# A Mamba block with a mixture of experts on one core: dt made by one Softplus activation in place of Abs, Relu, Exp, Ln and a GpSimd sum

## The reference

```python
xz = layernorm(x) @ W_in + b_in;  x_proj, z = split(xz)      # 256 and 256 channels
u = silu(x_proj)
B, C = split(u @ W_xproj + b_xproj)                          # 16 states each
dt = softplus(u @ W_dt + b_dt)                               # 256 channels
# for every channel d and state s, along the 512 steps:
h = h * exp(dt * A[d, s]) + (dt * u) * B[s]
y = sum_s h * C[s] + D * u
x = x + (y * silu(z)) @ W_out + b_out
# then softmax gates, top 2 of 8 experts and one shared expert, each
# silu(x @ w1.T) * (x @ w3.T) @ w2.T, scaled by its gate and summed; x = x + that
```

## Time and profile before

| | us |
|---|---|
| median of 3 runs | 1234.91 (1234.74 to 1237.38) |
| the profiled execution | 1235.3 |
| its span in the profile | 1233.3 |
| ACT busy | 1138.8 (92%) |
| PE busy | 1157.0 (94%) |
| DVE busy | 1130.1 (92%) |
| POOL busy | 1042.8 (85%) |

### The profile page before, as it was taken

The page is one execution under the profiler, slowest core; times in us unless marked ns, Lnnn a source line. Parts: engine busy times, 40 slices in busy tenths (PEclk is TensorE's granted clock), DMA queues, the critical chain, the costliest instruction groups (busy, mean ns, idle before and its releaser), DMA issues.

```text
span 1233.3 us, 21816 instructions
## 1 busy us (share of the span) xinstructions
PE 1157.0 (94%) x7200; PEld 946.7 (77%) x7200; DVE 1130.1 (92%) x1833; ACT 1138.8 (92%) x1982; POOL 1042.8 (85%) x534
## 2 busy tenths in 40 slices
PE   5466899999999999999999999999999999999998
PEld 3344576878888787878888787887878788888887
DVE  3788899999999999999999999999999999999754
ACT  6666999999999999999999999999999999989854
POOL 2999999999989999998999998999899899987300
PEclk8677999999999999999999999999999999999999
DMA  8333152506034160613325060433407043330000
GB/s 297 155 141 142 73 215 77 222 10 268 34 148 155 52 242 9 240 61 148 154 80 214 10 272 30 155 147 120 182 8 286 9 163 131 164 129 10 10 9 10
DMA packets 48016, 153.67 MB, mean 125 GB/s; under 512 B 4512, under 2 KB 29472, under 8 KB 31392
## 3 DMA queue, kind: packets, MB, share of 16 engines
q1 hardware_dynamic: 47904, 152.28, 31.9%
HBM read 147.03 MB, written 5.24 MB: 123 GB/s over the span
## 4 chain that ended last, share of the span: by engine, by line
ACT 50%; PE 26%; issue 10%; POOL 8%; DVE 4%; SPq 1%; DMA 1%; DVEq 0%; ACTq 0%; POOLq 0%
ACT da L661 13%; PE h L1021 13%; ACT L661 8%; ACT mixed L704 7%; ACT silu L697 6%; PE mixed L990 6%; PE y_acc L1003 5%; POOL dbu L754 4%; ACT L697 4%; DVE hc L856 3%; POOL hc L764 2%; ACT xn L677 1%; ACT xt L611 1%; ACT L642 1%; ACT lin L636 1%
## 5 line engine op out<-in xcount | busy, mean ns | idle before, releaser
L754 POOL TENSOR_TENSOR dbu<-w_s,b_all 128x1024 f32<-128x1024 f32 x256 | 604.3, 2383 | 2.1 <-DMA c_all<-bc_rows 2.1
L764 POOL TENSOR_TENSOR hc<-hc,c_all 128x1024 f32<-128x1024 f32 x128 | 304.6, 2380 | 92.0 <-DVE hc L856 91.6
L661 ACT ACTIVATE da<-dt_s,a_neg 128x512 f32<-128x512 f32 x512 | 342.1, 689 | 30.5 <-DVE hc L856 16.0
L1003 PE MATMUL y_acc<-ident,hc 128*128 128x128 f32 x2048 | 290.9, 279 | 35.8 <-POOL hc L764 25.0
L856 DVE TENSOR_TENSOR_SCAN hc<-da,dbu 128x512 f32<-128x512 f32 x256 | 302.2, 1211 | 18.6 <-ACT da L661 14.7
L856 DVE TENSOR_TENSOR_SCAN da<-da,dbu 128x512 f32<-128x512 f32 x256 | 308.1, 1216 | 10.4 <-POOL dbu L754 6.0
L1003 PEld LDWEIGHTS y_acc<-ident,hc 128*128 128x128 f32 x2048 | 246.5, 144 | 87.5 <-POOL hc L764 35.7
L990 PE MATMUL mixed<-w_s,g 128*128 128x128 f32 x2304 | 284.0, 276 | 4.6 <-DVE acc L906 1.8
L990 PEld LDWEIGHTS mixed<-w_s,g 128*128 128x128 f32 x2304 | 272.6, 192 | 20.0 <-DVE g L898 10.2
L1021 PE MATMUL h<-x_hi,w_hi 128*128 128x512 f32 x576 | 273.4, 475 | 9.6 <-ACT silu L697 6.2
L1021 PE MATMUL h<-x_hi,w_lo 128*128 128x512 f32 x576 | 228.2, 396 | 0.0
(11 more groups left out here) (79 smaller groups left out, 1039.3 us busy)
## 6 DMA issues: line engine op xcount, KB each, us to landing
b_all<-bc_rows SPq DMA_DIRECT2D x64, 1024.0 KB, 6.4
c_all<-bc_rows SPq DMA_DIRECT2D x64, 1024.0 KB, 8.8
xt<-in_x SPq DMA_DIRECT2D x16, 256.0 KB, 2.9
res<-in_x SPq DMA_DIRECT2D x16, 256.0 KB, 2.9
out<-acc SPq DMA_DIRECT2D x16, 256.0 KB, 4.3
silu<-in_w SPq DMA_DIRECT2D x6, 256.0 KB, 4.3
w_s<-in_w SPq DMA_DIRECT2D x1, 1152.0 KB, 7.3
bc_rows<-bc_rows_s SPq DMA_DIRECT2D x16, 64.0 KB, 1.6
```

Source lines behind the costliest of these rows:

```text
L661: act.activation(da[a % DA_SLOTS][:, :], dt_s[:, c, :], ACT.Exp, scale=a_neg[:, a:a + 1]).then_inc(decay_made, 1)
L754: pool.tensor_tensor(dbu[:, at:at + AT_ONCE, :], w_s[:, c, None, :].broadcast_to([P, AT_ONCE, T]), b_all[:, s:s + AT_ONCE, :], ALU.mult).t ...
L764: pool.tensor_tensor(pair, pair, c_all[:, s:s + 2, :], ALU.mult).then_inc(c_by_pool, 1)
L1003: last = pe.matmul(y_acc[:, b, :], hc[:, a % HC_SLOTS, b * P:(b + 1) * P], ident[:, :], is_transpose=True, start=False, stop=(a % NS == NS ...
```

## The change

Each half of dt is made by one Softplus activation out of the bank, straight into `dt_s`, which now has a slot for even and one for odd sequences. `softe`, `softl` and POOL's `dt` are taken out of all lists, the arrays `soft` and `lin` and three semaphores are gone, and nothing else is moved: `dlc.0` and `dlc.1` stand where they stood. Decays and w wait for the activation that frees the bank of `dl`. The activation waits (from sequence 2 on) until the sequence two before has made its decays and w of that half.

```diff
-        softe.0 decay.20-1 ycopy.0-1 decay.21-1 sc.5-3 softl.0 decay.22-1 decay.23-1 sc.6-3 bcc.0 decay.24-1
+        decay.20-1 ycopy.0-1 decay.21-1 sc.5-3 decay.22-1 decay.23-1 sc.6-3 bcc.0 decay.24-1
...
-        dbu.6+1 dbu.7+1 dt.1+1 w.1+1 rs2.0 hcp.10+1 dbu.8+1 dbu.9+1 hcp.14+1 dbu.10+1 hcp.18+1 dbu.11+1
-        dbu.12+1 dbu.13+1 dt.0+2 hcp.22+1 w.0+2 dbu.14+1
+        dbu.6+1 dbu.7+1 w.1+1 rs2.0 hcp.10+1 dbu.8+1 dbu.9+1 hcp.14+1 dbu.10+1 hcp.18+1 dbu.11+1
+        dbu.12+1 dbu.13+1 hcp.22+1 w.0+2 dbu.14+1
...
-        soft = sb("soft", [P, NC, T])
-        lin = sb("lin", [P, NC, T])
-        dt_s = sb("dt_s", [P, NC, T])
+        dt_s = sb("dt_s", [P, DT_SLOTS, NC, T])
...
                 elif what == "dlc":
-                    if not first:
-                        act.wait_ge(dt_made, NC * (m - 1) + a + 1)
-                    bias = bdt_s[:, a:a + 1]
-                    act.activation(soft[:, a, :], tile[:, :], ACT.Abs, bias=bias).then_inc(magnitudes, 1)
-                    act.activation(lin[:, a, :], tile[:, :], ACT.Relu, bias=bias).then_inc(freed, 1)
-                elif what == "softe":
-                    act.wait_ge(magnitudes, NC * (m + 1))
-                    act.activation(soft[:, :, :], soft[:, :, :], ACT.Exp, scale=-1.0).then_inc(soft_steps, 1)
-                elif what == "softl":
-                    act.wait_ge(soft_steps, 2 * m + 1)
-                    act.activation(soft[:, :, :], soft[:, :, :], ACT.Ln, bias=1.0).then_inc(soft_steps, 1)
+
+                    if m > 1:
+                        act.wait_ge(decay_made, STEPS * (m - 2) + NS * (a + 1))
+                        act.wait_ge(w_made, NC * (m - 2) + a + 1)
+                    act.activation(dt_s[:, m % DT_SLOTS, a, :], tile[:, :], ACT.Softplus,
+                                   bias=bdt_s[:, a:a + 1]).then_inc(freed, 1)
...
                 elif what == "decay":
-                        act.wait_ge(dt_made, NC * m + c + 1)
+                        act.wait_ge(*taken("dl", c, m))
...
-                elif what == "dt":
-                    pool.wait_ge(soft_steps, 2 * (m + 1))
-
-                    wait(pool, decay_made, STEPS * (m - 1) + NS * (a + 1))
-                    wait(pool, w_made, NC * (m - 1) + a + 1)
-                    pool.tensor_tensor(dt_s[:, a, :], soft[:, a, :], lin[:, a, :], ALU.add).then_inc(dt_made, 1)
                 elif what == "w":
-                    pool.wait_ge(dt_made, NC * m + a + 1)
+                    pool.wait_ge(*taken("dl", a, m))
```

More of the change, by code:

```diff
@@ L39 @@
 MIXED_BANKS, H_BANKS = 2, 3
+DT_SLOTS = 2
 SILU_SLOTS, G_SLOTS = 6, 3
@@ L120 @@
     "act": """
-        norm1.0 x_tc.0 u.0 u.1 whi.0 whi.1 whi.2 whi.3 bcc.0 whi.4 whi.5 dlc.0 dlc.1 softe.0 softl.0 whi.6
+        norm1.0 x_tc.0 u.0 u.1 whi.0 whi.1 whi.2 whi.3 bcc.0 whi.4 whi.5 dlc.0 dlc.1 whi.6
         whi.7 skip.0 whi.8 zs.0 decay.0 norm1.0+1 decay.1 decay.2 decay.3 decay.4 decay.5 decay.6 x_tc.0+1
         decay.7 decay.8 decay.9 zs.1 decay.10 decay.11 decay.12 decay.13 u.0+1 u.1+1 decay.14 decay.15
-        decay.16 dlc.0+1 decay.17 dlc.1+1 decay.18 ycopy.0 decay.19 softe.0+1 decay.20 softl.0+1 decay.21
+        decay.16 dlc.0+1 decay.17 dlc.1+1 decay.18 ycopy.0 decay.19 decay.20 decay.21
         decay.22 skip.0+1 bcc.0+1 decay.23 decay.24 decay.25 decay.26 decay.27 decay.28 decay.29 decay.30
@@ L128 @@
         decay.12+1 decay.13+1 silu.0 silu.1 u.0+2 u.1+2 silu.2 decay.14+1 decay.15+1 dlc.0+2 decay.16+1
-        dlc.1+2 decay.17+1 silu.3 decay.18+1 decay.19+1 ycopy.0+1 rexp.0 decay.20+1 softe.0+2 decay.21+1
-        softl.0+2 decay.22+1 decay.23+1 bcc.0+2 decay.24+1 decay.25+1 silu.4 silu.5 silu.6 silu.7 decay.26+1
+        dlc.1+2 decay.17+1 silu.3 decay.18+1 decay.19+1 ycopy.0+1 rexp.0 decay.20+1 decay.21+1
+        decay.22+1 decay.23+1 bcc.0+2 decay.24+1 decay.25+1 silu.4 silu.5 silu.6 silu.7 decay.26+1
         decay.27+1 skip.0+2 decay.28+1 decay.29+1 silu.8 decay.30+1 decay.31+1 sc.1 sc.2 decay.0+2 decay.1+2
@@ L134 @@
         sc.4 decay.12+2 decay.13+2 u.0+3 u.1+3 silu.15 silu.16 decay.14+2 decay.15+2 sc.5 decay.16+2 dlc.0+3
-        decay.17+2 silu.17 decay.18+2 bcc.0+3 decay.19+2 ycopy.0+2 decay.20+2 dlc.1+3 decay.21+2 softe.0+3
-        norm2.0+1 decay.22+2 decay.23+2 sc.6 decay.24+2 splitc.0+1 decay.25+2 xhi.0+1 softl.0+3 decay.26+2
+        decay.17+2 silu.17 decay.18+2 bcc.0+3 decay.19+2 ycopy.0+2 decay.20+2 dlc.1+3 decay.21+2
+        norm2.0+1 decay.22+2 decay.23+2 sc.6 decay.24+2 splitc.0+1 decay.25+2 xhi.0+1 decay.26+2
         sc.7 decay.27+2 decay.28+2 sc.8 decay.29+2 silu.0+1
@@ L167 @@
     "pool": """
-        rs1.0 resb.0 rs1.0+1 dt.0 dt.1 w.0 w.1 dbu.0 dbu.1 dbu.2 dbu.3 hcp.2 dbu.4 dbu.5 hcp.6 dbu.6 dbu.7
-        hcp.10 dbu.8 dbu.9 hcp.14 dbu.10 dbu.11 hcp.18 dbu.12 dbu.13 dbu.14 hcp.22 dbu.15 dt.0+1 hcp.26
+        rs1.0 resb.0 rs1.0+1 w.0 w.1 dbu.0 dbu.1 dbu.2 dbu.3 hcp.2 dbu.4 dbu.5 hcp.6 dbu.6 dbu.7
+        hcp.10 dbu.8 dbu.9 hcp.14 dbu.10 dbu.11 hcp.18 dbu.12 dbu.13 dbu.14 hcp.22 dbu.15 hcp.26
         w.0+1 rs1.0+2 dbu.0+1 hcp.30 dbu.1+1 dbu.2+1 dbu.3+1 hcp.2+1 dbu.4+1 rs2.0 dbu.5+1 hcp.6+1 dbu.6+1
[L171 to L175, removed]
+        w.1+1 hcp.10+1 dbu.7+1 dbu.8+1 dbu.9+1 hcp.14+1 dbu.10+1 rs1.0+3 hcp.18+1 dbu.11+1 dbu.12+1
+        dbu.13+1 hcp.22+1 dbu.14+1 w.0+2 hcp.26+1 dbu.15+1 dbu.0+2 hcp.30+1 dbu.1+2 dbu.2+2 dbu.3+2
+        hcp.2+2 resb.0+1 dbu.4+2 hcp.6+2 dbu.5+2 w.1+2 dbu.6+2 hcp.10+2 dbu.7+2 rs2.0+1 dbu.8+2
+        hcp.14+2 dbu.9+2 dbu.10+2 dbu.11+2 hcp.18+2 dbu.12+2 dbu.13+2 hcp.22+2 dbu.14+2 dbu.15+2
+        rs1.0+4 hcp.26+2 w.0+3 dbu.0+3 hcp.30+2 dbu.1+3 dbu.2+3 resb.0+2 hcp.2+3 dbu.3+3 dbu.4+3
         hcp.6+3 dbu.5+3 dbu.6+3 rs2.0+2 w.1+3 hcp.10+3 dbu.7+3 dbu.8+3 dbu.9+3 hcp.14+3 dbu.10+3 dbu.11+3
-        hcp.18+3 dbu.12+3 dt.0+4 w.0+4 dbu.13+3 hcp.22+3 dbu.14+3 dbu.15+3 rs1.0+5 hcp.26+3 dbu.0+4 dbu.1+4
-        hcp.30+3 dbu.2+4 dbu.3+4 dbu.4+4 resb.0+3 dt.1+4 hcp.2+4 dbu.5+4 hcp.6+4 w.1+4 dbu.6+4 dbu.7+4
-        rs2.0+3 hcp.10+4 dbu.8+4 dbu.9+4 dbu.10+4 hcp.14+4 dbu.11+4 hcp.18+4 dt.0+5 dbu.12+4 dbu.13+4
+        hcp.18+3 dbu.12+3 w.0+4 dbu.13+3 hcp.22+3 dbu.14+3 dbu.15+3 rs1.0+5 hcp.26+3 dbu.0+4 dbu.1+4
+        hcp.30+3 dbu.2+4 dbu.3+4 dbu.4+4 resb.0+3 hcp.2+4 dbu.5+4 hcp.6+4 w.1+4 dbu.6+4 dbu.7+4
+        rs2.0+3 hcp.10+4 dbu.8+4 dbu.9+4 dbu.10+4 hcp.14+4 dbu.11+4 hcp.18+4 dbu.12+4 dbu.13+4
         hcp.22+4 w.0+5 dbu.14+4
@@ L210 @@
         silu.14-4 silu.15-4 decay.14-2 decay.15-2 sc.4-4 decay.16-2 norm2.0-3 decay.17-2 dlc.0-1 decay.18-2
-        dlc.1-1 decay.19-2 ycopy.0-2 decay.20-2 softe.0-1 decay.21-2 sc.5-4 softl.0-1 decay.22-2 decay.23-2
+        dlc.1-1 decay.19-2 ycopy.0-2 decay.20-2 decay.21-2 sc.5-4 decay.22-2 decay.23-2
         sc.6-4 decay.24-2 bcc.0-1 decay.25-2 silu.16-4 sc.7-4 silu.17-4 decay.26-2 splitc.0-3 xhi.0-3
@@ L217 @@
         decay.13-1 u.0 silu.13-3 u.1 silu.14-3 silu.15-3 decay.14-1 decay.15-1 sc.4-3 decay.16-1 norm2.0-2
-        decay.17-1 dlc.0 decay.18-1 dlc.1 decay.19-1 ycopy.0-1 softe.0 decay.20-1 decay.21-1 sc.5-3 softl.0
+        decay.17-1 dlc.0 decay.18-1 dlc.1 decay.19-1 ycopy.0-1 decay.20-1 decay.21-1 sc.5-3
         decay.22-1 decay.23-1 sc.6-3 bcc.0 decay.24-1 decay.25-1 silu.16-3 sc.7-3 silu.17-3 decay.26-1
@@ L256 @@
     "pool": """
-        dbu.15-1 hcp.26-1 dbu.0 dbu.1 hcp.30-1 dbu.2 dbu.3 hcp.2 resb.0-1 dbu.4 dbu.5 hcp.6 dt.1 w.1 dbu.6
+        dbu.15-1 hcp.26-1 dbu.0 dbu.1 hcp.30-1 dbu.2 dbu.3 hcp.2 resb.0-1 dbu.4 dbu.5 hcp.6 w.1 dbu.6
         rs2.0-1 dbu.7 hcp.10 dbu.8 hcp.14 dbu.9 dbu.10 dbu.11 hcp.18 dbu.12 hcp.22 dbu.13 dbu.14 dbu.15
@@ L434, in build @@
         norm1_made = sem("norm1_made")
-        magnitudes = sem("magnitudes")
-        soft_steps = sem("soft_steps")
-        dt_made = sem("dt_made")
         w_made = sem("w_made")
@@ L660, in task @@
                             act.wait_ge(scanned, STEPS * (m - back) + user + 1)
-                    act.activation(da[a % DA_SLOTS][:, :], dt_s[:, c, :], ACT.Exp,
+                    act.activation(da[a % DA_SLOTS][:, :], dt_s[:, m % DT_SLOTS, c, :], ACT.Exp,
                                    scale=a_neg[:, a:a + 1]).then_inc(decay_made, 1)
@@ L731, in task @@
                                        ALU.add).then_inc(res_biased, 1)
-                elif what == "dt":
-                    pool.wait_ge(soft_steps, 2 * (m + 1))
-                    wait(pool, decay_made, STEPS * (m - 1) + NS * (a + 1))
-                    wait(pool, w_made, NC * (m - 1) + a + 1)
-                    pool.tensor_tensor(dt_s[:, a, :], soft[:, a, :], lin[:, a, :], ALU.add).then_inc(dt_made, 1)
                 elif what == "w":
-                    pool.wait_ge(dt_made, NC * m + a + 1)
+                    pool.wait_ge(*taken("dl", a, m))
                     pool.wait_ge(*taken("xp", a, m))
-                    pool.tensor_tensor(w_s[:, a, :], dt_s[:, a, :], u[:, a, :], ALU.mult).then_inc(w_made, 1)
```

(1 more changed line is left out.)

## The result

The change made the kernel slower: 1318.38 us median (1316.73 to 1318.58) against 1235.06, a ratio of 1.067 with a 95% interval of 1.066 to 1.068. Forecast were 1284.4 and a range of 1260 to 1302. The direction was right and so was the mechanism of the scans; the loss is 83 us where I had worked out 49.5.

A forecast was written before the change was run, and what follows sets the result against it. ACT's own work was taken to set the 70.97 us period. Window 41, sequence 15 3.5, sequences 1 to 4 10 and start -5 gave 49.5 on 1235.3: 1284.8, or 1284.4 beside the median; range 1260 to 1302.

The forecast's parts named there:

- the mechanism of the scans: Window: scans 18 and 19 wait 1.3 and 2.9 us for ACT's decays, leaving DVE 4.25 us late.
- (a): Window, sequences 5 to 14: each period grows by 4.1 us, 41 us in all.
- (b): Sequence 15: same lag of the scans, less DVE work between, estimated at 3.5 us.
- (c): Sequences 1 to 4: POOL's two saved sums pay for most of a lag; 0.4, 4, 3.3 and 2.6, 10 us.
- (d): Start, sequence 0: POOL's first w can start 5.7 us earlier; a gain of 5 us taken.
- Loads and Softplus: ACT, one dt: Softplus 0.68 us, two round trips with four loads; 6.7 to 6.8 us against 6.90 before.
- The lag: Window: scan 19 makes DVE 4.25 us late, then ACT idles 4.1 at decay.22 and decay.23; period 75.1 us.
- PE follows: Window: PE is late inside the same lag, as bc.0 needs the bank comb.5 leaves; no added cost.
- ACT's own work sets the period: Kernel before, window: ACT is never held up while DVE sometimes is, so ACT's work makes the 70.97 us.
- the ring: Window: ACT's decay.22 and decay.23 wait for DVE's mul.20 and mul.21, then ACT works 57.2 us without a wait.
- R1: Rival: DVE's lag is caught up and time follows ACT's sum of work, faster, 1228; chance 0.08.

The follow-up runs named there:

- e1: Changed kernel plus seven zero-weight multiplies on PE inside h3.14 in every sequence, filling PE's idle time: 1304.71 us, ratio 1.056.
- a1: Changed kernel with dlc.1 moved directly behind dlc.0 in all sequences but 3, one table round trip for two: 1265.44 us, ratio 1.024.
- b1: Changed kernel with DVE's g.12 moved ahead of scan.19, in the window's list alone: 1302.79 us, ratio 1.054.
- a2: Changed kernel with Abs in place of Softplus, so no table loads before it: 1233.04 us, ratio 0.998.
- e2: The a2 kernel with one of the three products of every expert unit left out on PE: 1219.39 us, ratio 0.988.
- b3: The b2 kernel with ACT's ycopy.0 moved ahead of dlc.1 in the window's list: 1301.97 us, ratio 1.054.
- b2: Changed kernel with DVE's g.12, g.13 and g.14 moved ahead of scan.19, in the window's list alone: 1300.89 us, ratio 1.053.

## Why the prediction was wrong in size

The growth of each interval from one `dlc.0` to the next, by step of the prediction:

| step | forecast us | measured us |
|---|---|---|
| (a) window, sequences 5 to 14 | 10 x 4.1 = 41 | 58.9 |
| (b) sequence 15 and what follows | 3.5 | 5.5 |
| (c) sequences 1 to 4 | 0.4 + 4 + 3.3 + 2.6 = 10 | 4.9 + 4.8 + 4.7 + 6.7 = 21.1 |
| (d) start | -5 | -2.3 |
| spans, 1316.5 - 1233.3 | 49.5 | 83.2 |

- **Loads and Softplus: right.** 0.687 us for a Softplus (0.68 taken), a load ahead of it and one at the decay behind, 1.30 and 2.0 us as steps, 29 loads more. The drain of about 1380 ns that the Trainium skill (ScalarE: Activation LUTs, What ACT_TABLE_LOAD costs) adds to each load is not seen here either: 1.29 us from the start of the load at 665.39 to the Softplus at 666.68.
- **The lag: right to a tenth.** Waits of 1.30 and 2.78 us at the scans, then ACT's at `decay.22` and `decay.23`. With PE's clock kept up (e1) the period is 75.12 for the 75.1 worked out, and with one round trip (a1) it is 72.86 for a lag of 1.87.
- **"PE follows": the step that failed.** I had PE late inside the same lag and gave it no price. It stops for 4.03 us at `h3.15`, whose bank `g.12` of DVE has to leave, comes back at half clock, is late with `eo.6`, and makes `g.15` wait, which stands ahead of `mul.21` in DVE's list and so on the very ring that sets the period. That is the term missing from (a): 1.8 us a sequence, shown by e1 and by the two periods of the changed kernel. Some two thirds of it pass through `g.15` (0.53 and 1.45 us of wait in turn). The other 0.5 us come after `decay.23`, most of it at `sc.7` of ACT, which waits 0.3 us for PE's product and waits for nothing in e1. The Trainium skill (TensorE: Matmul & The Clock Gate, Why this matters for your kernels) warns of idle gaps between bursts of multiplies, and the trace agrees: 0.50 behind 4.03 us.
- **(c), sequences 1 to 4: mis-sized.** I let POOL's saved sums pay for the lag at the start since POOL set the pace there. They did not: POOL itself now waits 3.09 us for scan 19 of sequence 0 (its `hcp.18` starts at 72.58 us), and is busy 35.41 of the 40 us from 40 to 80. In e1 these four intervals grow by 4.3, 3.1, 4.5 and 4.1 us, 5 less than here. Only sequence 4 (4.1 for 6.7) is the clock, which was at half here from 289 to 296 us and is not in e1. The other 2.4 e1 has lost ahead of them: both kernels reach the `dlc.0` of sequence 3 at 205 us. So of the 11 us missing 2.6 are the clock, and some 8.5, which e1 has too, are lag that I had discounted. The sizes in the first intervals are good to 3 us only: b1, whose edit lies in the window alone, reaches that `dlc.0` at 201.8.
- **(d), the start: mis-sized.** POOL's first dbu came 5.3 us earlier, but DVE's last weight subtractions took 2.06 us each beside POOL, where they had taken 0.64, and held the first scan (29.49 to 35.66). The price I allowed for was POOL's w being slow, not DVE. (b), the end, took 5.5 us for 3.5; that was not followed up.
- **"ACT's own work sets the period": wrong as a sentence, though the ring was worked out rightly.** a2 takes 5.3 us in 74 from ACT and wins 0.07 of a period. ACT never waited because DVE's work lay exactly under its gap at Ln; with the gap gone the wait appeared (2.89 and 1.10 us at `decay.22` and `decay.23`). The change itself didn't show this, as it left ACT's sum nearly alone. It speaks against R1 too, which let the time follow ACT's work.

Open: how PE's part and the ring share the floor of 70.9 us; e2 takes 0.5 us of it away, but with less PE work its idle gaps move as well. That e1's gain in the window is the clock, and not some other effect of keeping PE busy, rests on the granted clock staying at 1.00 with nothing else changed, and on the sequences with the same wait of PE and different clocks, in the changed kernel (1.1 us) and in b3 (0.7 us). Why the half clock lasts longer in some sequences than in others is not shown.

## What to carry to other kernels

In a schedule written out by hand, a saved microsecond can be worth nothing while the work laid under it stays in its place (a2: 5.3 us of ACT's work for 0.07 of a period). A gap that is moved costs its length where it now opens and gives nothing back where it was, as long as the filler still stands there (here some 4.1 us a sequence, with ACT's sum as before). Before replacing several activations by one from another table, ask for each use how many decays, copies or products wait behind it for the table to come back; two uses with a neighbour between them pay for two round trips (a period of 76.9 us, against 72.9 side by side). And follow every stall that a change makes on to PE: behind an idle gap PE can come back at half clock, and the late product can land on the path that was already the longest.

## What the runs showed of the hardware

- PE's granted clock after idle time: 1.00 after 1.72 us (a1), 0.66 over 5 us behind 2.42 (b2), 0.50 behind 4.03 (the changed kernel). Behind 2.29 us (b3) it fell in seven sequences and stayed at 1.00 in one, and near the end of b2's window it fell behind 1.81 us (0.50 from 1045.8 to 1049.2). So the length of the last wait alone does not tell whether the clock falls. Multiplies by zero weights, which left 0.97 us of idle time, kept it at 1.00 (e1).
- DVE's subtraction of two SBUF arrays (128 x 512) took 0.64 us beside POOL's sums and 2.06 beside POOL's products, while POOL's products took 2.66 in place of 2.33; in the kernel before it was POOL that was slow (2.6 us a sum in place of 1.29). DVE's products with one operand in a bank take some 0.68 us beside POOL all through the window. The Trainium skill (SBUF — State Buffer, Who interferes with whom) has it that a DVE instruction with two SBUF inputs contends with a GpSimd instruction that reads SBUF, and one with at most one, outside the modes that use two ports, does not; the rows agree.
